# A graph attention layer with a mixture-of-experts tail: the carried row handled later in the step, x rows gathered ahead for all chunks, and fewer gathers in the last step

## What is computed

```python
h = (layernorm(x) @ W).reshape(n, 4, 64)
alpha = leaky_relu(einsum(h, att_src)[src] + einsum(h, att_dst)[dst], 0.2)
alpha = exp(alpha - segment_max(alpha, dst)[dst])
alpha = alpha / (segment_sum(alpha, dst)[dst] + 1e-16)
out = segment_sum(alpha[:, :, None] * h[src], dst).reshape(n, 256) + bias
x = x + relu(layernorm(out) * gamma + beta)
# router on the mean row picks 2 of 8 experts for all rows
x = x + layernorm(experts(layernorm(x)) + layernorm(x)) * gamma + beta
```

## Time and profile before

| | us |
|---|---|
| median of 3 runs (lowest, highest) | 3504.13 (3502.38, 3505.12) |
| the profiled execution | 3474.59 |
| its span, first to last instruction | 3472.8 |
| mean granted TensorE clock | 0.855 |

### The profile page before, as it was taken

How to read it: one execution, slowest core, us unless ns; L and a number is a source line. 1 busy time by engine, 2 the same in 40 slices (tenths; PEclk the granted TensorE clock), 3 DMA queues, 4 the chain that set the end, 5 groups by cost and what they waited for, 6 DMA issues and landing times. The chain is left out here.

```text
span 3472.8 us, 66576 instructions
## 1 busy us (share of the span) xinstructions
PE 2494.7 (72%) x13162; PEld 1809.5 (52%) x13162; DVE 2261.4 (65%) x9525; ACT 1741.6 (50%) x5715; POOL 1606.7 (46%) x1689
## 2 busy tenths in 40 slices
PE   7746666766666766666666666666666699999998
PEld 6534445555554555454444444444444466666666
DVE  5446676766766667676666666666666655655555
ACT  4436666666665666665655555555555422222221
POOL 5465555655655656555666666666666000000000
PEclk9858888887778888888888888888888799999999
DMA  8944444444444444444444444444445201111110
GB/s 282 325 130 129 130 136 133 134 134 131 133 131 129 135 135 134 131 133 131 133 130 130 132 131 131 132 133 133 132 130 128 68 31 37 39 39 38 37 36 33
DMA packets 238971, 415.86 MB, mean 120 GB/s; under 512 B 67998, under 2 KB 153502, under 8 KB 238878
## 3 DMA queue, kind: packets, MB, share of 16 engines
q0 software_dynamic: 80064, 229.34, 24.9%
q1 hardware_dynamic: 157462, 184.01, 16.3%
q10 hardware_dynamic: 1351, 1.62, 0.2%
HBM read 361.68 MB, written 53.13 MB: 119 GB/s over the span
## 5 line engine op out<-in xcount | busy, mean ns | idle before, releaser
L781 POOL DMA_INDIRECT rows<-table,idx x1594 | 1526.3, 958 | 1008.6 <-issue 404.0
L874 PE MATMUL bank<-msg,oh 128*128 128x260 f32 x3332 | 984.7, 451 | 115.4 <-issue 99.4
L874 PEld LDWEIGHTS bank<-msg,oh 128*128 128x128 f32 x3332 | 750.5, 230 | 287.8 <-issue 134.1
L1105 ACT ACTIVATE msg<-rows,we 128x65 f32<-128x65 f32 x1904 | 478.6, 333 | 0.4
L1406 DVE TENSOR_TENSOR msg<-rows,bank 128x520 f32<-128x520 f32 x595 | 382.3, 677 | 0.6 <-DVEq L111 0.3
L992 PE MATMUL bank<-rows,msg 128*128 128x256 f32 x1536 | 340.6, 378 | 0.0
L979 PE MATMUL bank<-rows 128*128 128x512 f32 x768 | 335.8, 595 | 2.6 <-DMA rows<-in_L_ffn_W 2.6
L1098 ACT ACTIVATE oh_b<-bank 128x896 bf16<-128x896 bf16 x238 | 205.3, 914 | 244.3 <-remote 226.4
L922 PE MATMUL bank<-ident_b,ohT 128*128 128x128 bf16 x1666 | 178.8, 289 | 199.0 <-DVE acc L1553 52.0
L1241 ACT ACTIVATE msg<-bank,b_sb 128x512 f32<-128x512 f32 (+1 forms) x200 | 134.4, 679 | 364.4 <-PE bank L979 346.7
L992 PEld LDWEIGHTS bank<-rows,msg 128*128 128x128 f32 x1536 | 288.4, 189 | 51.4 <-issue 10.3
(11 more groups left out here) (223 smaller groups left out, 4108.8 us busy)
## 6 DMA issues: line engine op xcount, KB each, us to landing
dst_b<-dst SPq DMA_DIRECT2D x121, 448.0 KB
rows<-table,idx POOLq DMA_INDIRECT x1594
tab_w<-table SPq DMA_DIRECT2D x120, 134.5 KB
x_w<-in_x_rows SPq DMA_DIRECT2D x120, 128.0 KB
x_mid<-x_o SPq DMA_DIRECT2D x119, 128.0 KB
table<-msg SPq DMA_DIRECT2D x50, 269.0 KB
rows<-x_mid SPq DMA_DIRECT2D x26, 512.0 KB, 3.9
msg<-in_x_rows SPq DMA_DIRECT2D x51, 256.0 KB
```

Of the source, the lines that this page charges most:

```text
L781: pool.indirect_dma_start(rows[:, slot, t, :], None, table, bass.IndirectOffsetOnAxis(ap=idx[slot][:, t:t + 1], axis=0), bounds_check=None ...
L874: mm = pe.matmul(psA, oh[:, of, t, :], msg[:, of, t, :], start=(t == 0), stop=(t == TILES - 1))
L1105: ins = act.activation(head_cols(msg[:, s, t, :])[:, h, :], head_cols(rows[:, at.slot(), t, 0:HC1])[:, h, :], ACT.Copy, scale=we[:, t, h:h ...
```

## The change

- The last-tile x rows are gathered and stored in stage 1 for all 119 chunks, not 74. Every step of stage 2 then has 13 table gathers and the x path (xrow, xT, and their load), and the two loops of steps become one.
- On ACT the copy of the carried row moves from before msgs0 to behind oh*, and rexp and carried behind it; acc and oh* come first.
- On DVE r_t, r_sc, r_mn, r_d1 and r_d move from among the messages to between MTILE* and MAXSELF*.
- On PE the x tile is turned without a wait for ACT's carry; expand* waits for ACT's xT instead of the carry product.
- For the last chunk 9 tiles are gathered (`LAST_TILES`); four DMAs of one number each raise the semaphore in place of the others. Their tiles hold only padding edges.

```diff
--- before.py
+++ after.py
@@ -153,9 +153,7 @@
...
     XO_ROWS = (GROUPS + 1) * GROUP
-    X_ROUNDS = (3 * PAIRS // 2 - 5) // RING
-    X_CHUNKS = X_ROUNDS * RING + 6
-    assert 0 < X_ROUNDS < SURE and X_CHUNKS <= chunks and X_CHUNKS <= 3 * PAIRS // 2 + 2
+    LAST_TILES = -(-(E - (chunks - 1) * CHUNK) // P)
...
@@ -391,7 +390,7 @@
...
         psC, psZ = bank[5][0:1, 0:AW], bank[7][0:1, 0:D + 1]
-        psXT = [bank[5][:, 320:320 + P], bank[6][:, 328:328 + P]]
+        psXT = [bank[3][:, 352:352 + P], bank[6][:, 328:328 + P]]
         psXR = bank[6][:, 64:64 + D + H]
...
@@ -469,14 +465,14 @@
...
         def pair_ahead(c):
-            return (c - 2) * 2 // 3
+            return (c - 2) * PAIRS // chunks
...
@@ -738,18 +732,18 @@
...
             pool.wait_ge(s_xidx, 16)
-            for c in range(X_CHUNKS // 3):
+            for c in range(chunks // 3):
                 gather_x(c)
...
             pool.tensor_scalar(narrow, wide, float(TOP16), None, ALU.min).then_inc(s_narrow, 1)
-            for c in range(X_CHUNKS // 3, X_CHUNKS):
+            for c in range(chunks // 3, chunks):
                 gather_x(c)
...
-            def gather(at, lo, hi, repeated=False, cell=0):
+            def gather(at, lo, hi, repeated=False, cell=0, filled=TILES):
@@ -771,23 +765,24 @@
...
                     pool.tensor_tensor(turn[:, cell:cell + 1], turn[:, 2:3], turn[:, 2:3], ALU.add).then_inc(s_turn, 1)
-                n_tiles = GATHERS if hi > 2 else TILES
-                for t in range(n_tiles):
+                for t in range(GATHERS):
                     if t == FIRST_ROW:
...
                             pool.tensor_tensor(turn[:, cell + 1:cell + 2], turn[:, 2:3], turn[:, 2:3], ALU.add).then_inc(s_turn, 1)
+                    if t >= filled:
+                        pool.dma_start(spare[0:1, t:t + 1], src_t[0:1, t:t + 1]).then_inc(s_rows[slot], 16)
+                        continue
                     pool.indirect_dma_start(rows[:, slot, t, :], None, table,
...
             for n in range(-4, SURE * RING + 1):
-                first_steps = n < X_ROUNDS * RING + 3
-                gather(At(0, RING, n), -n if n < 1 else -2, 5 if first_steps else 2)
+                gather(At(0, RING, n), -n if n < 1 else -2, 5)
             pool.sem_inc(s_turn, 2)
             far_rounds(pool, total, lambda at, lo, hi: gather(at, lo, hi, repeated=True))
-            gather(behind(total)[0], -2, 1, repeated=True, cell=3)
+            gather(behind(total)[0], -2, 1, repeated=True, cell=3, filled=LAST_TILES)
@@ -905,7 +900,6 @@
...
                     dve2.wait(pe, MSGS[-1], at)
-                    act2.wait(pe, "carry", at)
                     act2.wait(pe, "xT", at, -1)
@@ -924,6 +918,8 @@
...
                 if ahead:
+                    if to_turn:
+                        act2.wait(pe, "xT", at)
                     dve2.wait(pe, "LO*", at)
@@ -943,7 +939,6 @@
...
                     act2.wait(pe, "carry", at)
-                    act2.wait(pe, "xT", at)
                     pe2.mark("carry", pe.matmul(psC, sel[:, at.slot(-1):at.slot(-1) + 1], acc[:, :], start=True, stop=True))
...
@@ -1120,18 +1115,13 @@
...
                     act2.skip(act, ["we", "we_act"], at)
-                if before:
-                    pe2.wait(act, "carry", at, -1)
-                    act2.mark("carry", act.activation(carry[:, :], psC, ACT.Copy))
-                else:
-                    act2.skip(act, ["carry"], at)
                 if own:
...
                 if far:
-                    act.wait_ge(s_rows[at.slot(2)], rows_landed(at, 2, hi))
+                    act.wait_ge(s_rows[at.slot(2)], rows_landed(at, 2))
                     act2.wait(act, "xrow", at, -1)
@@ -1143,12 +1133,25 @@
...
                 if prev:
-                    dve2.wait(act, "r_d", at)
-                    act2.mark("rexp", act.activation(r_f[:, :], r_d[:, :], ACT.Exp))
                     pe2.wait(act, "agg", at)
...
                     act2.mark("acc", act.activation(acc[:, 0:HC1], psA, ACT.Copy))
+                else:
+                    act2.skip(act, ["acc"], at)
+                if ahead:
+                    pe2.wait(act, "agg", at)
+                    act2.mark("oh*", copy_one_hots(oh[:, q, :, :]))
+                else:
+                    act2.skip(act, ["oh*"], at)
+                if before:
+                    pe2.wait(act, "carry", at, -1)
+                    act2.mark("carry", act.activation(carry[:, :], psC, ACT.Copy))
+                else:
+                    act2.skip(act, ["carry"], at)
+                if prev:
+                    dve2.wait(act, "r_d", at)
+                    act2.mark("rexp", act.activation(r_f[:, :], r_d[:, :], ACT.Exp))
                     act2.wait(act, "rexp", at)
@@ -1156,12 +1159,7 @@
...
                 else:
-                    act2.skip(act, ["rexp", "acc", "carried"], at)
-                if ahead:
-                    pe2.wait(act, "agg", at)
-                    act2.mark("oh*", copy_one_hots(oh[:, q, :, :]))
-                else:
-                    act2.skip(act, ["oh*"], at)
+                    act2.skip(act, ["rexp", "carried"], at)
                 if to_row:
@@ -1478,26 +1476,15 @@
...
                 mark(before, "mv_m", lambda: dve.bn_aggr(x_o[:, s, D:D + 2], st2[:, :]))
-                for name in MSGS[1:4]:
+                for name in MSGS[1:]:
                     message(name)
-                if prev:
-                    act2.wait(dve, "carry", at)
-                mark(prev, "r_t", lambda: dve.tensor_scalar(r_t[:, :], carry[:, HAS:HAS + 1], BIG, -BIG, ALU.mult, ALU.add))
-                message(MSGS[4])
                 mark(far, "wcur^", lambda: dve.tensor_copy(wcur[:, s, :], w_tab[:, bass.ds(at.number(2), 2)]))
-                done("r_t")
-                mark(prev, "r_sc", lambda: dve.tensor_scalar(r_sc, carry[:, SHIFT:HAS], r_t[:, 0:1], None, ALU.add))
                 if far:
...
                     newseg[:, s, 1:P], dst_s[:, s, 1:P], dst_s[:, s, 0:P - 1], ALU.not_equal))
-                done("r_sc")
-                mark(prev, "r_mn", lambda: dve.tensor_tensor(r_mn, r_sc, adsh[0:1, q4, H:], ALU.max))
                 done("wcur^")
                 mark(far, "node^", lambda: dve.tensor_tensor(node[:, s:s + 1], iota_col[:, :], wcur[:, s, 0:1], ALU.add))
-                done("r_mn")
-                mark(prev, "r_d1", lambda: dve.tensor_tensor(r_d[:, 0:H], r_sc, r_mn, ALU.subtract))
-                mark(prev, "r_d", lambda: dve.tensor_tensor(r_d[:, H:], adsh[0:1, q4, H:], r_mn, ALU.subtract))
                 if beside:
@@ -1518,17 +1505,27 @@
...
                     mtile[:, :, :], node_v[:, :, 1:R5], over(nohas[:, :], H), ALU.add))
+                if prev:
+                    act2.wait(dve, "carry", at)
+                mark(prev, "r_t", lambda: dve.tensor_scalar(r_t[:, :], carry[:, HAS:HAS + 1], BIG, -BIG, ALU.mult, ALU.add))
                 if far:
...
                 mark(far, "ohT0^", lambda: one_hots(0))
+                done("r_t")
+                mark(prev, "r_sc", lambda: dve.tensor_scalar(r_sc, carry[:, SHIFT:HAS], r_t[:, 0:1], None, ALU.add))
                 done("MTILE*")
...
                     mnode[:, :], mtile[:, :, :].rearrange("p t h -> p h t"), X, ALU.max))
+                done("r_sc")
+                mark(prev, "r_mn", lambda: dve.tensor_tensor(r_mn, r_sc, adsh[0:1, q4, H:], ALU.max))
                 if ahead:
...
                 mark(ahead, "AD*", lambda: dve.tensor_copy(adsh[:, n4, 0:H], tab_w[:, n4, AD:TW]))
+                done("r_mn")
+                mark(prev, "r_d1", lambda: dve.tensor_tensor(r_d[:, 0:H], r_sc, r_mn, ALU.subtract))
+                mark(prev, "r_d", lambda: dve.tensor_tensor(r_d[:, H:], adsh[0:1, q4, H:], r_mn, ALU.subtract))
                 done("MNODE*")
```

More of the change, by code:

```diff
@@ L303, in build @@
         wide = flat_rows[:, 0:EP].bitcast(I32)
-        x_idx = flat_oh[:, 0:X_CHUNKS * TILES].bitcast(I32)
+        x_idx = flat_oh[:, 0:chunks * TILES].bitcast(I32)
         assert 2 * EP <= GATHERS * TW
-        x_parts = [slice(i, min(i + X_BATCH, X_CHUNKS)) for i in range(0, X_CHUNKS, X_BATCH)]
+        x_parts = [slice(i, min(i + X_BATCH, chunks)) for i in range(0, chunks, X_BATCH)]
         x_ring = X_SLOT * (RING - 1) // X_BATCH
@@ L362, in build @@
         dve2 = Ticks(sem("dve2"), """
-            EDGE_V self_z ZE self_l LE SEL* D MASK* DMIN self_d LAST_HI* LAST_R* LAST_MID* MPEN* LAST_LO* st_m msg0 mv_m msg1 msg2 msg3 r_t msg4
-            wcur^ r_sc newseg^ r_mn node^ r_d1 r_d pen^ NODE_V* RUNMAX^ NOHAS* LASTMAX^ MTILE* ohT0^ MNODE* AD* MAXSELF* ohT^ ZN*
+            EDGE_V self_z ZE self_l LE SEL* D MASK* DMIN self_d LAST_HI* LAST_R* LAST_MID* MPEN* LAST_LO* st_m msg0 mv_m msg1 msg2 msg3 msg4
+            wcur^ newseg^ node^ pen^ NODE_V* RUNMAX^ NOHAS* LASTMAX^ MTILE* r_t ohT0^ r_sc MNODE* r_mn AD* r_d1 r_d MAXSELF* ohT^ ZN*
             accshift SHIFT* mergedshift HI* REST* MID* merged0 merged1 LO* merged2 merged3 den rden
```

(13 more changed lines are left out.)

23 lines of the change are left out of this document (11 added, 12 removed).

## The result

The changed kernel takes 3547.26 us (median of 4 runs, 3540.34 to 3555.81), the kernel before 3503.87 beside it: a ratio of 1.0124, 95% interval 1.0103 to 1.0146, 43 us slower. Forecast were 3411 us.

What follows compares the result with a forecast made beforehand. A step was taken as bound by a ring of waits, with POOL ending last in late steps. From 3504.1 us, steps -118, stage 1 +27 and last gather -2 gave 3411 us; range 3360 to 3525.

Steps and rivals of the forecast that it cites:

- The working rule: Stage 2: PE's marks become visible to others 1.5 to 2 us after POOL stops gathering, and late before.
- The wait of ACT for carry: ACT's wait for the late carry mark, 2.82 us in the step shown, should vanish and stand before acc.
- the longer chain: DVE from lT's mark to merged: 5.0 us instead of 3.4, so the chain grows by 1.6 us.
- The wait ahead of r_t: On DVE a wait for ACT's carry before r_t should appear, of about 1 us.
- The pause for lT: POOL's pause in early steps should fall from 3.13 to 2.04 us, 1.1 us a step in 70 steps.
- Is the rest of the ring short enough?: DVE's ring of 18.0 us plus 1.6 minus 0.4 leaves 0.7 us slack; 0.3 us added to the floor.
- Rival B: Carried row's chain on DVE ends last, delayed by late marks: steps of 22.0 us, whole 3618 us; chance 0.14.
- Stage 1: Gathering and storing x rows for 45 more chunks before the steps costs +27 us, bounds 20 and 34.
- The 14th gather: Dropping one gather and one gap on POOL saves 1.25 us in each of 45 late steps.
- The last gather: Four gathers fall away for four one-element DMAs on POOL's queue: 0 to 5 us gained once, taken as -2.
- The sum: Whole kernel: -118 + 27 - 2 = -93 us, from 3504.1 to 3411 us.
- The floor: Stage 2 step bound by POOL's 13 gathers and two pauses: 19.9 us, forecast 20.2; bounds 19.9 and 22.0.

Runs made afterwards that it cites:

- six_again: Changed kernel without the gathers of tiles 6 to 12 in the steps once buffers are filled (wrong sums), beside before at 3474.64 us: 3156.39 us, ratio 0.9074.
- changed3: The changed kernel itself once more, beside before at 3474.64 us: 3478.64 us, ratio 1.0016.
- before7: Kernel before with one gather moved in front of the wait for lT (7 and 6, late steps 7 and 7): ratio 1.0009 to before at 3507.55 us.
- order7: Changed kernel's new order, 7 gathers behind expand* and 6 behind lT, x rows for 74 chunks only: ratio 1.0159 to before at 2961.45 us.
- thin: Changed kernel with the x gathers of the last 44 chunks cut to 16 of 256 numbers a row (wrong values): ratio 1.0126 to before.
- carry_mid: Changed kernel with ACT's copy of the carried row between acc and oh* instead of behind oh*: 2926.46 us, ratio 0.9884 to before.
- xrows: Kernel before plus only x rows for all 119 chunks, 13 gathers per step, one loop, last gather cut; old order: 3487.57 us, ratio 1.0055.
- mid7_74: Changed kernel with ACT's carried-row copy between acc and oh*, 7 gathers behind expand*, x rows for 74 chunks only: ratio 0.9984 to before at 2965.64 us.
- again: The changed kernel itself once more, beside before at 3507.55 us: ratio 1.0128.
- first7: Changed kernel with one gather moved in front of the wait for lT, 7 and 6 instead of 6 and 7: 3425.74 us, ratio 0.9874 to before.
- first7_again: Changed kernel with 7 gathers behind expand* and 6 behind lT, once more, beside before at 2965.64 us: ratio 1.0131.

## Why the prediction was wrong, step by step

**The working rule** (marks come late until POOL stops) was right on chips B, and `six_again` shows it; chips A look the same, and on chips C the idle time from den to st is 0.14 us. **The wait of ACT for carry** vanished, and **the longer chain** has its forecast length, 4.9 against 5.0 us. **The wait ahead of r_t** is there, 44.3 us in 49 steps. **The pause for lT** didn't fall: counted from xmid lT does come sooner, but xmid comes later (the table below).

**The step that failed** is "Is the rest of the ring short enough?". I added the chain's 1.6 us to DVE's 18.0, subtracted 0.4, found a slack of 0.7 us and gave 0.3 us for steps in which DVE ends last. Two things were wrong in it. First, the 18.0 us come from one step of 19.9 us. In the mean an early step of before takes 21.2 us and DVE waits 1.24 us ahead of NODE_V, so its ring is 20.0 us, and with 1.2 us more it fills the whole 21.2: there was no slack. Second, merged, den, rden and biased moved from 3.4 us behind lT to 4.9 and more, into the very time in which I had read late marks. Their waits and st's grew by 3.18 - 1.11 = 2.1 us (1.7 on a chip B), and no term of the sum held them. What the runs show in its place is DVE's ring ending last. Means between the starts of DVE's rows, steps 8 to 60, in us:

| | before (B) | `changed3` (B) | `six_again` (B) | `before7` (A) | changed (A) | `order7` (C) |
|---|---|---|---|---|---|---|
| NODE_V to merged | 3.37 | 5.04 | 4.29 | 3.47 | 4.78 | 5.06 |
| merged to st | 3.92 | 5.01 | 2.30 | 4.89 | 5.67 | 2.32 |
| st to xmid | 3.91 | 2.10 | 2.04 | 2.30 | 2.04 | 2.04 |
| xmid to the next NODE_V | 10.01 | 8.59 | 9.53 | 10.91 | 8.97 | 7.63 |
| wait ahead of NODE_V, part of the line above | 1.24 | 0.62 | 0.26 | 0.64 | 0.19 | 0.03 |

On chips B the way to the merged rows grew by 1.7 us, as forecast, and the one to st by 1.1. Of this 1.4 us came back ahead of NODE_V, where ACT no longer waits for carry (1.1 was forecast), and 1.8 us between st and xmid: late marks for which DVE had waited there before. Ahead of gam it idled 102.2 us in all and now 4.0 (first before, then the changed kernel):

```profile
L1588 DVE SCALAR_TENSOR_TENSOR o<-o,mv,g_aff 128x256 f32<-128x256 f32 x115 | 55.7, 484 | 102.2 <-remote 56.3 <-DVE mv L1584 24.7 <-issue 10.4
L1585 DVE SCALAR_TENSOR_TENSOR o<-o,mv,g_aff 128x256 f32<-128x256 f32 x115 | 56.2, 489 | 4.0
```

So the late marks in part only changed places, and the step fell by 0.46 us instead of 1.0.

Rival B had the mechanism and the place, and I gave it 0.14. Its sum, with the measured 2.1 us in place of 2.8, gives 18.0 - 0.4 + 1.6 + 2.1 = 21.3 us, against 21.45, but that is luck: it starts from the short step and leaves out the waits that vanish behind st. My argument against it was that late marks end with POOL's run. They do (st starts 1.5 us behind it in `changed3`), but before, st had come 2.6 us ahead of that end, so the delay was long all the same.

All three marks of failure that I had named were met: POOL's pause for lT is 3.6 us, the first output came later than 300 us, and DVE waits for lT ahead of NODE_V in 33 steps only, 34.0 us in all. A chip like the one of the profile would not have saved the forecast: on chips B the ratio is 1.0016, and 3411/3504 is 0.973.

**Stage 1** was mis-sized as well: 27 us forecast, 43 and 45 measured on chips B (305.1 and 307.4 against 262.6), 46 on A (311.7 against the 266.1 of `before7`). I took bytes over bandwidth, let the bytes fill the free DMA time, and let POOL's 56 us go into its waits. Little of either happened. The DMA share of the first 100 us is 0.88 as before, and in 100 to 150 us it fell from 1.01 to 0.95. POOL had (147.8 - 10.6) - 73 x 1.25 = 46 us of waits, and in the changed kernel, with the last x gather at 193.5, there still are 34. Only 12 us were filled. What is left are mostly waits for PE's marks of the pairs (17.1 us for L802, 8.6 for L823); why the pairs come slower on chips A and B isn't shown. On chips C (167.5 - 11.8) - 118 x 1.25 = 8 us are left, the last gather follows POOL's pace, and the first output comes 23 to 25 us later than with 74 chunks: near the forecast, but in part by luck, as `thin` gives the bytes only a part of it. A rule that I weighed, of the Trainium skill, "DMA: Bandwidth & Descriptors", section Bandwidth (358 GB/s bind between HBM and SBUF), decides nothing here, and the measurement goes above it: `carry_mid` has 382 GB/s in 50 to 100 us, with one core at work.

**The 14th gather** was to save 1.25 us in 45 steps. `xrows` shows 0.43 on a chip B, where late marks hold the step; `mid7_74` against `carry_mid` the full 1.3 on C, where the chain is shorter than POOL. **The last gather** was to save 2 us: from the 116th row of x_mid to the last it took 43.4 us before and 43.8 in `xrows`. Nothing can be seen of it.

**The sum.** On chips B: start +45, steps 70 x (20.74 - 21.17) + 45 x (20.71 - 21.32) = -58 by the profiles, where -118 was forecast; the medians say +4 in all, and profiles stray from them by up to 25 us. On chips A 41 to 43 us are lost and the start costs 46, so by the medians the steps give next to nothing back. By the profiles of `again` and `before7` they give 34 us, but the one lies 10 us below its median and the other 15 above. That split rests on `before7` in place of before, which wasn't profiled on such a chip.

**The floor**: 20.2 us forecast, 20.30 and 20.17 in `first7`, one more edit on. It holds for chips B only, as POOL's two pauses of 2 us come with the late marks: on chips C they are gone, and `carry_mid` has 16.44 us.

## What to carry to other kernels

Before a chain is moved, list the waits that lie behind it as well, and ask of each whether it moves into a time in which marks come late; a slack of 0.7 us is none if three operations behind it can wait 0.7 us each. Take a ring's length from the mean over the steps and not from one of them: here one step said 18.0 us and the mean 20.0. Where one engine works in runs between two waits, where the run is cut is a parameter of its own, to be tried again whenever the order around it changes: here it turned a loss of 0.2% into a gain of 1.3% on one kind of chip, and next to nothing on another (on chips like the first it wasn't run). And compare two profiles only if the kernel before ran as fast beside both.

## What the runs showed of the hardware

- The same kernel took 2961, 3472 and 3508 us on different chips, with the same durations of its operations (RECIPROCAL 178 ns, a gather 0.95 us; DVE's operations sum to 18.96 us a step both in `changed3` and in `first7_again`). The difference lies between operations, and only where POOL gathers: from the last row of x_mid to the end, where POOL does nothing, it is 725.1 us in before, 726.4 in the changed kernel (A) and 724.8 in `order7` (C). Steps of before take 21.2 us on B; those of the changed kernel 21.5 on A, 20.7 on B, and 17.1 on C with the split of `first7`. What distinguishes the chips can't be seen in a trace.
- Late marks need POOL's gathers (idle time 2.81 us in `changed3`, 0.14 in `six_again`). They hit DVE's waits on its own marks as well as those of others. The Trainium skill, "Perfetto Trace Analysis", section "Summary: the profiler window per engine type", says that the spreading of a semaphore lies outside the profiled window. The traces agree: RECIPROCAL and BATCH_NORM_STATS2 keep their 178 and 427 ns where they wait, the gaps ahead of them grow.
- A few small copies of DVE do take longer beside the gathers, on both kinds of chip: this one 253 ns in `changed3` and 296 in `first7_again`, and 157 in `six_again`. First `changed3`, then `six_again`:

```profile
L1541 DVE COPY acc<-r_m 1x4 f32<-1x4 f32 x115 | 29.1, 253 | 0.4
L1543 DVE COPY acc<-r_m 1x4 f32<-1x4 f32 x115 | 18.1, 157 | 0.0
```

  The Trainium skill's "Trainium Architecture — The Big Picture", section "What this means for kernel authors", has DVE and GpSimd contend for a shared port pair. That would fit the copies, but with 0.3 us a step in all (DVE's operations sum to 18.62 us in `six_again`) it isn't the lateness: the copies are longer on chips C too, where DVE doesn't wait.
- PE's granted clock, a mean of its two levels with 1 for 2.4 GHz, was 0.82 over the early steps before, 0.78 in the changed kernel and 0.87 in `carry_mid`. How much of a step this is worth wasn't tried.
